# Second layer of a two-layer convolution and attention kernel: VectorE taps ordered by chunk pairs, offset products inside a query group, fewer position steps, one normalisation a step later

## The reference, cut to what matters

```
x_ln    = layernorm(x, ln_g, ln_b)                # viewed again as (b, c, h, w)
q       = x_ln @ wq + bq
o       = depthwise_conv(q, dw_w, 7x7, stride 2, pad 3)      # 16x16 positions, 49 taps
o       = gelu(o + dw_b, exact)
offsets = conv1x1(o, pw_w)                        # 2 numbers for each of 256 positions
grid    = (refs + tanh(offsets) + 1) * (h / R) / 2           # y and x, then to pixels
interp  = bilinear sample of x at grid            # 256 rows of 512 channels
k = v   = interp @ wv + bv
att     = softmax(heads(q @ mq + b) @ heads(k @ mk + b)^T) @ heads(v @ mv + b)
z       = att @ mo + mo_b + x
out     = gelu(layernorm(z) @ mlp + mlp_b) + z
```

## Time and profile before

| what | value |
|---|---|
| median of 3 runs | 3982.0 us (3978.45 to 3982.71) |
| the profiled execution, its own time | 3974.67 us |
| its span, first to last instruction | 3972.9 us |
| TensorE matmul busy | 3804.8 us (96%) |
| VectorE busy | 2958.0 us (74%) |
| ScalarE busy | 2429.9 us (61%) |
| GpSimd busy | 1640.2 us (41%) |

### The profile page before, as it was taken

The page is one execution under the profiler, slowest core; times in us unless marked ns, Lnnn a source line. Parts: engine busy times, 40 slices in busy tenths (PEclk is TensorE's granted clock), DMA queues, the critical chain, the costliest instruction groups (busy, mean ns, idle before and its releaser), DMA issues. The chain is left out here.

```text
span 3972.9 us, 63406 instructions
## 1 busy us (share of the span) xinstructions
PE 3804.8 (96%) x21614; PEld 3185.7 (80%) x21614; DVE 2958.0 (74%) x5158; ACT 2429.9 (61%) x5241; POOL 1640.2 (41%) x1935
## 2 busy tenths in 40 slices
PE   8999999999999999999999899999999999999999
PEld 6887888888888878878888757777777777777777
DVE  3983984975966948939849657888887878788876
ACT  3873864855846837828738526565656555555656
POOL 1432432423432433324325315554545455555554
PEclk9999999999999999999999999999999999999999
DMA  2231331241331321322312323131313131323221
GB/s 88 54 78 41 66 75 45 57 92 35 59 86 40 57 76 42 64 66 55 81 48 57 90 82 85 64 85 64 85 64 85 65 85 64 78 69 80 70 74 57
DMA packets 175079, 269.31 MB, mean 68 GB/s; under 512 B 58732, under 2 KB 91560, under 8 KB 174760
## 3 DMA queue, kind: packets, MB, share of 16 engines
q1 hardware_dynamic: 170152, 248.48, 25.4%
q0 software_dynamic: 4608, 16.78, 1.3%
HBM read 113.90 MB, written 33.82 MB: 37 GB/s over the span
## 5 line engine op out<-in xcount | busy, mean ns | idle before, releaser
L647 DVE TENSOR_REDUCE a_neg_max<-a_ps 128x1 f32<-128x1024 f32 x512 | 622.0, 1216 | 303.7 <-PE a_ps L481 303.7
L605 ACT ACTIVATE a_ph<-a_ps 128x512 fp32r<-128x512 f32 x1024 | 564.6, 597 | 190.2 <-PE a_ps L495 188.8
L664 DVE TENSOR_TENSOR a_pl<-a_ps,a_ph 128x512 fp32r<-128x512 f32 x1024 | 654.3, 679 | 6.2 <-ACT a_ph L605 2.8
L749 POOL TENSOR_TENSOR a_qk<-a_fold_s,a_fold_r 64x256 f32<-64x256 f32 x256 | 191.5, 748 | 1043.5 <-DVE a_fold_s L655 817.0
L612 ACT ACTIVATE a_prob<-a_ps,a_neg_max 128x1024 f32<-128x1024 f32 x512 | 572.5, 1118 | 31.7 <-DVE a_neg_max L647 31.7
L495 PE MATMUL a_ps<-a_ident,a_prob 128*128 128x128 f32 x4096 | 553.5, 276 | 38.2 <-DVE a_pl L664 37.1
L495 PEld LDWEIGHTS a_ps<-a_ident,a_prob 128*128 128x128 f32 x4096 | 460.0, 140 | 158.0 <-issue 94.4
L510 PE MATMUL a_ps<-a_ph,a_v 128*128 128x256 f32 x2048 | 550.7, 302 | 0.0
L510 PE MATMUL a_ps<-a_pl,a_v 128*128 128x256 f32 x2048 | 509.7, 282 | 0.0
L481 PE MATMUL a_ps<-a_kl,a_qs 128*128 128x512 f32 x1024 | 404.9, 395 | 0.0
L480 PE MATMUL a_ps<-a_kh,a_qs 128*128 128x512 f32 x1024 | 403.1, 394 | 0.0
(11 more groups left out here) (262 smaller groups left out, 9197.3 us busy)
## 6 DMA issues: line engine op xcount, KB each, us to landing
a_qs<-a_qk SPq DMA_DIRECT2D x128, 256.0 KB, 4.3
a_kl<-a_qk SPq DMA_DIRECT2D x128, 256.0 KB, 4.8
a_xtok<-in_x SPq DMA_DIRECT2D x64, 256.0 KB, 5.3
a_fold_r<-a_inv_row SPq DMA_DIRECT2D x256, 64.0 KB, 3.4
b_xs<-x SPq DMA_DIRECT2D x64, 256.0 KB, 4.5
b_qs<-b_qh SPq DMA_DIRECT2D x64, 256.0 KB, 3.1
b_qs<-b_ql SPq DMA_DIRECT2D x64, 256.0 KB, 3.8
b_z<-x SPq DMA_DIRECT2D x64, 256.0 KB, 3.3
```

The source lines that it names most:

```text
L605: act.activation(ph[:, b % 2, 4 * g:4 * g + 4, (u % 2) * P:(u % 2 + 1) * P], ps[:, 4 + n % 2, :].rearrange("p (k q) -> p k q", k=4), ACT.C ...
L647: dve.tensor_reduce(neg_max[:, i_:i_ + 1], ps[:, 2 * (i_ % 2):2 * (i_ % 2) + 2, :] .rearrange("p a b -> p (a b)"), AX, ALU.max, negate=Tru ...
L664: dve.tensor_tensor(pl[here], ps[:, 4 + n % 2, :].rearrange("p (k q) -> p k q", k=4), raw(ph[here]), ALU.subtract).then_inc(pl_ok, 1)
```

## The change

Four things change, all in layer 1.

1. **Order of the VectorE taps.** After the 20 solo taps the list now goes: chunk 0 in turn with chunk 1 until chunk 0's taps are out; then chunk 1 (with the sums of chunks 0 and 1 at its end) in turn with one tap of chunk 2 or 3; then chunks 2 and 3 in turn, with their sums. It has 104 entries as before. `POOL_SUM` of chunks 0, 1, 2, 3 was entry 61, 104, 102, 103 and is now entry 69, 73, 103, 104. Before, 20 entries have the chunk's former entry right ahead of them, 40 have it three back and 40 four back. Now 22 have it right ahead, 57 two back, 20 four back and one 28 back.
2. **Offset products.** Query group 2 goes to PSUM bank 6 and waits for the sums of chunk 1. The offset products of chunks 0 and 1 are made inside query group 2 (two after its 6th matmul, two after its 12th), those of chunks 2 and 3 after it. The two output columns of each half of the positions are now in banks 0 and 1.
3. **Positions.** `ref` is scaled ahead of all images, and VectorE computes the lower corner straight from Tanh's output: four instructions ahead of the index instead of seven. `pos` itself is made behind the index.
4. **`LN_AT`.** Tile 4 is normalised in step 8 instead of 7, tile 5 in step 9 instead of 8. Step 9 has two tiles, step 7 one.

```diff
+    left = [[(c, n) for n in range(first_dve[c], first_pe[c])] for c in range(CT)]
+    sums = [[(c, PE_SUM), (c, POOL_SUM)] for c in range(CT)]
     taps = [left[0].pop(0) for _ in range(SOLO)]
-    while any(left):
-        for l in [l for l in left if l][:4]:
-            taps.append(l.pop(0))
+    while left[0]:
+        taps += [left[0].pop(0), left[1].pop(0)]
+    left[1] += sums[1]
+    for n, m in enumerate(sums[0]):
+        left[1].insert(len(left[1]) - 3 + n, m)
+    while left[1]:
+        taps += [left[1].pop(0), left[2 + len(left[1]) % 2].pop(0)]
+    left[2] += sums[2]
+    left[3] += sums[3]
+    while left[2] or left[3]:
+        taps += [l.pop(0) for l in left[2:] if l]
...
+                dve.tensor_scalar(ref[:], ref[:], 1.0, HW / 2 / 2.0, ALU.add, ALU.mult).then_inc(chn, 1)
+                dve.wait_ge(chn, 10)
+                dve.tensor_scalar(ref[:], ref[:], 1.0, HALF_EDGE, ALU.add, ALU.mult).then_inc(chn, 1)
+                dve.wait_ge(chn, 11)
+                dve.tensor_scalar(ref_low[:], ref[:], 0.5, None, ALU.subtract).then_inc(chn, 1)
...
-        QH_BANK = (4, 5, 0, 7, 2, 3, 4, 5)
-        OFF_BANK = 1
+        QH_BANK = (4, 5, 6, 7, 2, 3, 4, 5)
+        OFF_BANK = (0, 1)
...
-        LN_AT = {4: (0,), 5: (1,), 6: (2,), 7: (3, 4), 8: (5,), 9: (6,), 10: (7,)}
+        LN_AT = {4: (0,), 5: (1,), 6: (2,), 7: (3,), 8: (4,), 9: (5, 6), 10: (7,)}
...
+            def offsets(k):
+
+                pe.wait_ge(gelu_ok, at(gelu_ok, k + 1))
+                for st in range(KT):
+                    mm = pe.matmul(ps[:, OFF_BANK[st], 0:2], o[:, k, st * P:(st + 1) * P],
+                                   vec[:, 20:28].rearrange("p (c k) -> p c k", c=2)[:, :, k],
+                                   start=k == 0, stop=k == CT - 1)
+                if k == CT - 1:
+                    mm.then_inc(off_ps, 1)
...
-                        pe.wait_ge(tap, at(tap, taps_upto[0]))
+                        pe.wait_ge(tap, at(tap, taps_upto[1]))
...
-                    mm.then_inc(qh_ps, 1)
+                        if k == CT - 1:
+                            mm.then_inc(qh_ps, 1)
+                        if g == 2 and k % 2 == 1:
+                            offsets(k // 2)
...
-            pe.wait_ge(tap, at(tap, taps_upto[1]))
-            for st in range(KT):
-                for k in range(CT):
-                    if st == 0:
-                        pe.wait_ge(gelu_ok, at(gelu_ok, k + 1))
-                    mm = pe.matmul(ps[:, OFF_BANK, 2 * st:2 * st + 2], o[:, k, st * P:(st + 1) * P],
-                                   vec[:, 20:28].rearrange("p (c k) -> p c k", c=2)[:, :, k],
-                                   start=k == 0, stop=k == CT - 1)
-            mm.then_inc(off_ps, 1)
+            offsets(2)
+            offsets(3)
             queries(range(3, 8))
...
             dve.wait_ge(tanh_ok, at(tanh_ok, 1))
-            dve.tensor_tensor(pos[:], pos[:], ref[:], ALU.add).then_inc(pos_ok, 1)
+            reach = HW / 2 / 2.0 * HALF_EDGE
+            dve.scalar_tensor_tensor(low_at[:], turned[:], reach, ref_low[:], ALU.mult, ALU.add).then_inc(pos_ok, 1)
...
             for y in range(2):
                 dve.tensor_scalar(idx[:, y, :], row_at[:], float(TOK * r + HW * y), None, ALU.add).then_inc(idx_ok, 1)
+            dve.scalar_tensor_tensor(pos[:], turned[:], reach, ref[:], ALU.mult, ALU.add).then_inc(pos_ok, 1)
             query(1)
```

More of the change, by code:

```diff
@@ L37 @@
 WHOLE = float(2 ** 23)
+HALF_EDGE = 0.5 * (HW - 1)
 class Region:
@@ L819, in layer1 @@
     first_pe = [POOL_TAPS[c] + DVE_TAPS[c] for c in range(CT)]
-    left = [[(c, n) for n in range(first_dve[c], first_pe[c])] + [(c, PE_SUM), (c, POOL_SUM)] for c in range(CT)]
+    left = [[(c, n) for n in range(first_dve[c], first_pe[c])] for c in range(CT)]
+    sums = [[(c, PE_SUM), (c, POOL_SUM)] for c in range(CT)]
     taps = [left[0].pop(0) for _ in range(SOLO)]
-    while any(left):
-        for l in [l for l in left if l][:4]:
-            taps.append(l.pop(0))
+    while left[0]:
[9 more added lines that the diff above has]
+        taps += [l.pop(0) for l in left[2:] if l]
     tap_before = [max([m + 1 for m in range(k) if taps[m][0] == taps[k][0]], default=0) for k in range(len(taps))]
@@ L849, in layer1 @@
         ref = R.take("b_ref", [P, 2, KT])
+        ref_low = R.take("b_ref_low", [P, 2, KT])
+        turned = R.take("b_turned", [P, 2, KT])
         pos = R.take("b_pos", [P, 2, KT])
@@ L1180, in _ @@
                    .then_inc(chn, 1)
+                dve.wait_ge(chn, 9)
+                dve.tensor_scalar(ref[:], ref[:], 1.0, HW / 2 / 2.0, ALU.add, ALU.mult).then_inc(chn, 1)
[3 more added lines that the diff above has]
+                dve.tensor_scalar(ref_low[:], ref[:], 0.5, None, ALU.subtract).then_inc(chn, 1)
                 dve.wait_ge(pe_s, 23)
@@ L1525, in scalar_image @@
             act.wait_ge(off_ps, at(off_ps, 1))
-            act.activation(pos[:], ps[:, OFF_BANK, 0:2 * KT].rearrange("p (s c) -> p c s", c=2), ACT.Tanh)\
+            act.activation(turned[:], ps[:, 0:2, 0:2].rearrange("p s c -> p c s"), ACT.Tanh)\
                .then_inc(tanh_ok, 1)
@@ L1681, in vector_image @@
             dve.wait_ge(tanh_ok, at(tanh_ok, 1))
-            dve.tensor_tensor(pos[:], pos[:], ref[:], ALU.add).then_inc(pos_ok, 1)
+            reach = HW / 2 / 2.0 * HALF_EDGE
+            dve.scalar_tensor_tensor(low_at[:], turned[:], reach, ref_low[:], ALU.mult, ALU.add).then_inc(pos_ok, 1)
             dve.wait_ge(pos_ok, at(pos_ok, 1))
-            dve.tensor_scalar(pos[:], pos[:], 1.0, HW / 2 / 2.0, ALU.add, ALU.mult).then_inc(pos_ok, 1)
+            dve.tensor_scalar(low_at[:], low_at[:], WHOLE, WHOLE, ALU.add, ALU.max).then_inc(pos_ok, 1)
             dve.wait_ge(pos_ok, at(pos_ok, 2))
-            dve.tensor_scalar(pos[:], pos[:], 1.0, 0.5 * (HW - 1), ALU.add, ALU.mult).then_inc(pos_ok, 1)
+            dve.tensor_scalar(low_at[:], low_at[:], WHOLE + HW - 2, WHOLE, ALU.min, ALU.subtract).then_inc(pos_ok, 1)
             dve.wait_ge(pos_ok, at(pos_ok, 3))
[L1688 to L1693, removed]
             dve.scalar_tensor_tensor(row_at[:], low_at[:, 0, :], float(HW), low_at[:, 1, :], ALU.mult, ALU.add)\
                .then_inc(pos_ok, 1)
-            dve.wait_ge(pos_ok, at(pos_ok, 7))
+            dve.wait_ge(pos_ok, at(pos_ok, 4))
             for y in range(2):
                 dve.tensor_scalar(idx[:, y, :], row_at[:], float(TOK * r + HW * y), None, ALU.add).then_inc(idx_ok, 1)
+            dve.scalar_tensor_tensor(pos[:], turned[:], reach, ref[:], ALU.mult, ALU.add).then_inc(pos_ok, 1)
             query(1)
+            dve.wait_ge(pos_ok, at(pos_ok, 5))
             dve.tensor_tensor(near[:, 0], pos[:], low_at[:], ALU.subtract).then_inc(near_ok, 1)
```

2 lines of the change are left out of this document (1 added, 1 removed).

## The result

| | before | after |
|---|---|---|
| median of 19 runs each | 3980.96 us (3974.3 to 3994.63) | **3970.3 us** (3959.69 to 3978.73) |
| ratio | | **0.9975, 95% interval 0.9967 to 0.9982** |
| profiled execution, its own time | 3974.67 us | 3967.28 us |
| span of it | 3972.9 us | 3965.6 us |

The account below looks back on a forecast made before the run. TensorE, busy 96% of the span, was taken as the bound, gains coming from its waits and low clock. Terms -4.8 + 4.9 - 9.6 - 2.0 - 7.8 = -19.3 us gave 3963 us, range 3953 to 3976.

Parts of the forecast that it names:

- LN_AT: MLP steps 7 to 9: TensorE's 1.17 us wait goes, 0.69 us reaches the convolution's end in 7 images, -4.8 us.
- step 9 is too full: Rival, MLP step 9: VectorE's wait can't absorb the second normalising pair, low parts slip, 3978 us; chance 0.10.
- Tap order: VectorE's convolution taps: entries behind their own chunk +0.26, moved sum +0.35 us an image, +4.9 us in 8 images.
- Entries two back: The 57 taps whose chunk's former entry is two back: taken to cost nothing more than 0.394 us each.
- the pair order stalls VectorE: Rival, the 57 entries two back: each costs up to 0.131 us more, +60 us, about 4020 us; chance 0.06.
- Tail and offsets: Convolution's end to query group 3: 1.2 us less than 2.53 in each of 8 images, -9.6 us.
- The change doesn't do what it says: Rival, query group 2: Gelus of chunks 0 and 1, or bank 6, hold TensorE, time as falls stay; chance 0.01.
- Positions: Steps ahead of the index: gathers 0.4 us earlier, less wait for the keys in some five images, -2.0 us.
- Clock: TensorE about the offsets: little-work stretch 2.2 us, clock falls in about half of images 1 to 7, -7.8 us.
- the falls stay: Rival, TensorE's clock about the offsets: small products and waits remain, no clock gain, -9.9 us, 3972 us; chance 0.21.

Follow-up runs that it names:

- the filled wait: The changed kernel with the first six matmuls of query group 2 done twice, results the same: 3953.93 us, ratio 0.994.
- the swap at the scores: Second part of value projection 0 put ahead of an image's first scores, against the kernel with the sums behind GpSimd's end: 3949.6 us against 3947.23.
- three taps fewer: The changed kernel with one tap each of chunks 1, 2 and 3 moved from VectorE to TensorE: 3954.09 us, ratio 0.9945.
- the fastest kernel: The changed kernel with POOL_SUM of chunks 0 and 1 late, group 2 awaiting chunk 1's PE_SUM, one chunk 3 tap on TensorE: 3949.86 us, ratio 0.9929.

## Why the prediction was right, and where it was not

1. **LN_AT: right.** -6.0 us without falls for -4.8. The rival *step 9 is too full* is out: VectorE's wait in step 9 is still 1.70 us, but it ends 1.49 us earlier (2757.62, not 2759.11), which makes room for the second pair, and the bias add keeps its time. What the prediction calls the first write of the padded image is the fifth; the 0.69 us stand all the same.
2. **Tap order: mis-sized, the step that failed.** "There the sum of chunk 0 held VectorE 0.69 us ... +0.35": I priced the sum that moves at 0.69, by the one row that showed a meeting, and left chunk 0's at the same price. Both measured 0.95 to 1.06. How long such a sum takes depends on when in GpSimd's instruction it comes, and the one row was a short case, 0.40 us into an instruction of 0.73. +10.0 us instead of +4.9.
3. **Entries two back: right.** They cost next to nothing, 0.40 us a tap; the rival *the pair order stalls VectorE* is out. The prediction's "never starts before the pipe is empty" goes beyond the rows: taps of 0.48 us that don't depend on each other start 0.39 us apart, the next one ahead of the former one's end.
4. **Tail and offsets: right**, 1.36 us an image for 1.2. *The change doesn't do what it says* is out. No run has this edit alone.
5. **Positions: right as an edit, wrong as a gain.** The index comes 0.28 us earlier behind Tanh, but key product to scores is 3.4 us longer in all: TensorE waits more for the keys' input (+1.4) and the keys' copy (+1.8). The first is the early arrival: it stands in images 0 and 2, the two with no fall at the offsets. The second is not. The copy is longest in images 4, 5 and 7, where TensorE came late to the keys, and it is the transfer itself that is slower: its first part `b_kl` takes 2.06 us from issue to landing in images 0 and 1, where TensorE waits 1.5 us, and 3.46, 2.96 and 3.16 us in images 4, 5 and 7, where it waits 2.85, 2.40 and 2.57. Before, images 5 and 7 had such a slow transfer too (3.41 and 3.01 us). What slows it is open. The sum had no term for it.
6. **Clock: right number by luck.** About the offsets the falls cost 8.2 us less, with 7.8 forecast; 3.5 x 1.2 + 2.4 is 6.6 and not "near 6", so the term itself should have been 7.2, and the sum 18.7. But the stretch was 3.1 us, not 2.2 ("2818.3 ... 2820.5"), because Q came 0.4 us later than I took and the products of chunk 1 0.5 us earlier. I had half of images 1 to 7 fall, and image 0 for 6.8 us; six of the seven fell, one of them for 6.8 us, and image 0 did not fall at all. The falls became shorter rather than gone. And four falls at the scores, 0.8 to 1.4 us each, 4.8 in all, stand in no term: I treated the falls as belonging to the offsets. Other kernels here fall at the scores too; what brings it on in one image and not in the next is open.
7. Of the rivals, *the falls stay* was nearest in time (3972). Its reason, small products and waits still there, is what the filled wait confirms; in shape it was wrong, since the falls shortened and new ones came elsewhere.

The range held, but with little to spare: 3976 was its slow end. The misses, 5.1, 4.8 and 5.4 us, are each small beside it, and all three had one sign: a meeting that was dearer than its row, falls at a place with no term, and waits for the keys' input and copy with no term.

## What to carry to other kernels

When VectorE and GpSimd share a stretch, place VectorE's sums of two SBUF tensors where GpSimd is idle or done, and price a meeting at the whole of GpSimd's instruction at least, not at the one row that happened to be short; one list here paid for two. When a change brings TensorE early to a fixed point, work out the wait it will find there. If the clock falls behind that wait, give TensorE more work ahead of it, at best a share of the other engine's: two taps did here what useless matmuls did, some 14 us each. And look one stage on: the softmax chain gave back all that the swap at the scores had won.

## What the runs showed that I had not expected

- Eleven us of useless matmuls made the kernel some 14 us faster (0.9975 to 0.994), for the most part by keeping the clock at 2.4 GHz where TensorE had waited 1.67 us.
- The same sum takes 0.34 us from start to start with GpSimd idle, and with GpSimd busy 0.61 to 0.71 (before), 0.95 to 1.06 (after) or 1.80 to 1.85 us (three taps fewer), and GpSimd's own product grows from 0.51 to 0.79 us.
- In layer 1 of the fastest kernel no image falls at the offsets and most do at the scores, and it still gains 0.7% on the kernel before.
